# A decoder layer's last stage reordered: a new order for the last four joins, other filler counts, duplicate marks in one piece, and gates without a gather

## The chip, the cores and the metric
One core of one Trainium2 chip runs the program. The metric is its device time in microseconds, the median over executions.

## What is computed
A decoder layer on x of 2048 tokens by 256: self-attention with line coordinates, cross-attention over 1601 context rows, and a mixture of 16 experts. The change lies in the last part:

```python
x = x + _L0_xattn_ref(_layernorm(x), ctx, ctx, Wq, Wk, Wv, Wo, bo)
x = x + _L0_ffn_ref(_layernorm(x), gate_query, log_temp, w1, b1, w2, b2)
# _L0_ffn_ref
affinity = _sinkhorn(einsum('bnd,ed->ben', x, gate_query) / exp(log_temp))   # 6 rounds
gates, idx = top_k(affinity, 64)                     # 64 tokens for each of 16 experts
expert_in = take_along_axis(x[:, None], idx[..., None], axis=2)
h = gelu(einsum('becd,edf->becf', expert_in, w1) + b1)                # 256 to 1024
expert_out = einsum('becf,efd->becd', h, w2) + b2                     # 1024 to 256
out = out.at[..., idx].add(gates[..., None] * expert_out)
```

## The kernel before
**The attention part.** `build_plan` writes one list of steps, and every engine goes through that list in order and does its own share of it. A planner picks each next step from ten streams, by estimated durations and weights. The steps of normalised rows, joins and queries are one stream, `x`, whose own order `join` writes out. A join of a block of 128 tokens is: `o_turn` (TensorE turns the attention output, L1861; VectorE divides by the sums into `attn`, L1439 and L1440), `a_turn` (TensorE turns `attn`, L1865; a copy to `attn_t`, L1444), `out_proj` (TensorE, L1871; VectorE adds it to the residual rows `xb`, L1450, and takes their statistics, L1271 to L1273; GpSimd raises the variance to the power -0.5, L1022), `norm` (VectorE, L1327, then a store to DRAM), `x_turn` (TensorE, L1821; a copy to `xn_t`, L1339) and `gate` (TensorE, L1899; a copy to `logits`, L1489). TensorE's results for these go through three banks `g` in turn: a step waits until the bank of three steps before has been read. The plain copies (`a_turn`, `x_turn`, `gate`) can be VectorE's or ScalarE's, as the planner picks; ScalarE costs 50 more once the scores have begun (`act_late`), so VectorE has them. The last four blocks (12 to 15) are joined after the last attention work, when nothing else is left in the plan.

**Fillers.** `keep_busy(n)` issues n matmuls of 128x256 in f32 that nobody reads (L1787; each shows as two in the trace). They stand after each late `out_proj` (3) and ahead of TensorE's waits in the router.

**The router.** After the plan, VectorE scales the logits and makes six Sinkhorn rounds with a column sum by TensorE in each. Then 128 chunks (8 for each expert) give their 64 largest values (`best_v`, eight at a time) and their places (`find_places`, L1567); the largest of an expert's candidates give a limit, which TensorE spreads (L1947); counts per chunk (L1952, L1953) give each chunk an offset. Six steps by powers of two (L1619, L1620) shift each chunk's indices to that offset, and a matmul (L1957) sums the chunks: `idx_gather`, 64 tokens of the two experts of a pair on 128 partitions, eight pairs.

**Duplicates.** A token can be chosen by both experts of a pair, and a scatter may not add to one row twice. For each pair `mark` makes a diagonal of the indices and a row of marks (L1640, L1641), a matmul with ones adds them over the partitions (L2008, `pair_sum`), `read_sums` compares (L1648, L1650), and `place_rows` (L1656 to L1664) builds the matrix `mix` and the rows of the scatter, with an unused token for the second copy.

**The experts.** For each pair: gather 128 rows (GpSimd, L1090), turn them (L1964), hidden layer (L1977) and b1 (L1677), turn (L1990), gelu (ScalarE), output layer (L2001) and b2 (L1693), `mix` scaled by the gates (L1684) and multiplied (L2019), a copy (ScalarE, L1229), a scatter with addition to DRAM (GpSimd, L1107), each after the one before. The gates come from DRAM too: SyncE stores the affinities (L983) and GpSimd gathers 16 of them for each token (L1098), behind each gather of rows. The order at the start is written out by hand: marks 0 to 3, rows of pairs 0 and 1, hidden 0, marks 4 and 5, rows 2, marks 6 and 7, hidden 1. Weights go through eight slots; SyncE asks for experts 3 to 7 after the last stores of the joins, and for experts 8 to 15 as slots come free (w1, L793, after a pair's hidden layer has been read; w2, L798, after its output has).

## Time and profile before

| | us |
|---|---|
| median of 3 executions (1174.15 to 1175.01) | 1174.94 |
| the profiled execution's own time | 1175.17 |
| its span | 1173.4 |
| TensorE busy | 1105.5 (94%) |
| VectorE busy | 860.9 (73%) |
| ScalarE busy | 718.2 (61%) |
| GpSimd busy | 151.4 (13%) |
| mean granted TensorE clock | 0.976 |

The attention part ends at 1007.5 us of the span, so what the change touches lies in the last 166 us. Busy time of TensorE there is partly fillers. The granted clock is 1.00 at 2.4 GHz and 0.50 at 1.2 GHz.

### The profile page before, as it was taken

What the parts mean: (1) busy time and instruction counts of PE and PEld (TensorE: products, weight loads), DVE (VectorE), ACT (ScalarE), POOL (GpSimd) and SP (SyncE); (2) the same over time, 40 slices, a digit from 0 to 9 for tenths busy, and PEclk for the clock granted to TensorE, in tenths of its full rate; (3) what the DMA queues carried; (4) which work ended last, traced back from release to release, by engine and by line L of the source; (5) the groups of instructions that cost most, each with busy time, mean ns of one, the idle gap of its engine ahead of it and who ended that gap; (6) DMA issues with size and microseconds to landing.
All of it is one profiled execution on the core that took longest, in us unless ns stands there. A gap on an engine that the chain in (4) does not pass through costs nothing.

```text
span 1173.4 us, 30372 instructions
## 1 busy us (share of the span) xinstructions
PE 1105.5 (94%) x12600; PEld 525.7 (45%) x12600; DVE 860.9 (73%) x2017; ACT 718.2 (61%) x823; POOL 151.4 (13%) x260
## 2 busy tenths in 40 slices
PE   4788999999999999999999999999999999888997
PEld 2443433332432323544454456555555552467554
DVE  4888565487788878889788889788878980378631
ACT  0345567887678867677776877677785789310111
POOL 3024125112111011000001000010001000000522
PEclk9898999999999989999999999999999999998999
DMA  5113408722011000103232200111102000088696
GB/s 168 32 36 95 117 16 152 169 36 74 25 35 40 16 15 2 53 28 88 79 101 65 88 18 28 52 47 30 30 20 65 17 16 2 24 310 193 184 345 173
DMA packets 81562, 90.45 MB, mean 77 GB/s; under 512 B 18208, under 2 KB 73952, under 8 KB 81424
## 3 DMA queue, kind: packets, MB, share of 16 engines
q1 hardware_dynamic: 75264, 80.04, 23.9%
q10 hardware_dynamic: 4368, 6.29, 1.7%
q0 software_dynamic: 1792, 2.16, 1.0%
q8 instruction: 100, 1.64, 0.6%
q14 instruction: 38, 0.31, 0.1%
HBM read 73.42 MB, written 15.04 MB: 75 GB/s over the span
## 4 chain that ended last, share of the span: by engine, by line
PE 76%; DVE 11%; DMA 5%; issue 4%; ACT 2%; POOL 1%; ACTq 0%; DVEq 0%; POOLq 0%
PE po L1778 24%; PE g L1886 16%; PE scores L1754 15%; PE scores L1758 6%; PE g L1871 3%; PE g L1831 2%; ACT probs L1194 2%; DMA out<-self_region,idx_scatter 1%; DVE mx L1465 1%; PE g L1821 1%; PE g L1861 1%; DMA out<-wo_sb,idx_scatter 1%; PE scores L1787 1%; DMA out<-wxq_sb,idx_scatter 1%; PE g L1977 1%
## 5 line engine op out<-in xcount | busy, mean ns | idle before, releaser
L1194 ACT ACTIVATE probs<-scores 128x1024 f32<-128x1024 f32 (+2 forms) x736 | 677.0, 968 | 239.7 <-PE scores L1754 131.3
L1465 DVE TENSOR_REDUCE mx<-g 128x1 f32<-128x400 f32 (+1 forms) x1024 | 526.4, 567 | 86.2 <-PE g L1886 76.6
L1886 PE MATMUL g<-cross_region,even_region 96*32 96x400 bf16 (+1 forms) x4096 | 310.5, 338 | 0.4
L1754 PE MATMUL scores<-even_region,cross_region 99*32 99x512 bf16 (+1 forms) x3264 | 255.0, 379 | 2.5 <-ACT probs L1194 2.5
L1778 PE MATMUL po<-probs,cross_region 128*32 128x512 f32 (+1 forms) x1664 | 225.3, 594 | 0.8 <-ACT probs L1194 0.8
L1886 PEld LDWEIGHTS g<-cross_region,even_region 96*32 96x32 bf16 x4096 | 123.3, 95 | 182.9 <-DVE mx L1465 81.9
L1778 PE MATMUL po<-probs,self_region 128*32 128x512 f32 (+3 forms) x1280 | 152.1, 550 | 4.5 <-POOL probs L1055 3.9
L1754 PEld LDWEIGHTS scores<-even_region,cross_region 99*32 99x32 bf16 (+1 forms) x3264 | 100.9, 96 | 96.0 <-issue 42.6
L1758 PE MATMUL scores<-self_region 36*128 36x512 bf16 (+3 forms) x640 | 104.9, 360 | 7.2 <-ACT probs L1194 6.8
L1055 POOL TENSOR_SCALAR_AFFINE_SELECT probs<-probs 128x256 f32<-128x256 f32 x128 | 58.8, 468 | 276.7 <-ACT probs L1194 275.9
L1022 POOL TENSOR_TENSOR rstd<-mv,half 128x1 f32<-128x1 f32 x48 | 26.7, 556 | 518.5 <-DVE mv L1273 518.3
L1758 PEld LDWEIGHTS scores<-self_region 36*128 36x128 bf16 x640 | 26.6, 94 | 126.1 <-ACT probs L1194 76.9
L1778 PEld LDWEIGHTS po<-probs,cross_region 128*32 128x32 f32 (+1 forms) x1664 | 56.8, 110 | 24.9 <-ACT probs L1194 6.4
L1224 ACT ACTIVATE even_region<-scores 128x1024 f32<-128x1024 f32 x4 | 4.1, 1026 | 85.8 <-PE scores L1990 85.8
L1787 PE MATMUL scores<-xbo_sb,ident 128*128 128x256 f32 x190 | 51.4, 424 | 0.0
L1778 PEld LDWEIGHTS po<-probs,self_region 128*32 128x32 f32 x1280 | 30.9, 110 | 33.6 <-POOL probs L1055 13.5
L1821 PE MATMUL g<-ident,xn 128*128 128x128 f32 x96 | 21.0, 305 | 25.7 <-DVE xn L1327 25.6
L1787 PEld LDWEIGHTS scores<-xbo_sb,ident 128*128 128x128 f32 x190 | 39.5, 214 | 6.3 <-issue 0.2
L1439 DVE RECIPROCAL rsum<-g 128x16 f32<-128x16 f32 x32 | 8.2, 255 | 45.7 <-PE g L1861 45.5
L1831 PE MATMUL g<-wself_sb,xn_t 128*128 128x512 f32 x64 | 34.3, 662 | 0.1
L1450 DVE TENSOR_TENSOR xb<-g,xb 128x256 f32<-128x256 f32 x32 | 13.6, 424 | 28.1 <-PE g L1871 27.3
L1821 PEld LDWEIGHTS g<-ident,xn 128*128 128x128 f32 x96 | 10.4, 146 | 42.9 <-issue 31.0
(287 smaller groups left out, 881.3 us busy)
## 6 DMA issues: line engine op xcount, KB each, us to landing
cross_region<-in_w SPq DMA_DIRECT2D x16, 1024.0 KB, 12.8
even_region<-xq_d SPq DMA_DIRECT2D x192, 64.0 KB, 2.3
self_region<-in_w ACTq DMA_DIRECT2D x6, 1024.0 KB, 6.6
self_region<-in_w SPq DMA_DIRECT2D x6, 1024.0 KB, 13.8
cross_region<-xk_d SPq DMA_DIRECT2D x24, 200.1 KB, 8.0
xb<-in_x SPq DMA_DIRECT2D x32, 128.0 KB, 2.8
xb<-x_d SPq DMA_DIRECT2D x32, 128.0 KB, 2.4
probs<-in_w SPq DMA_DIRECT2D x4, 1024.0 KB, 13.2
```

The lines of the kernel that those rows point to most:

```text
L1022: pool.tensor_tensor(rstd[:, u % 4:u % 4 + 1], mv[:, u % 4, 1:2], half[:, 0:1], ALU.pow).then_inc(rstd_ready, 1)
L1055: pool.affine_select(out=d, in_=d, compare_op=ALU.is_ge, fill=0.0, base=0, pattern=[[0, 2], [1, P]], channel_multiplier=-1).then_inc(mask_ ...
L1194: act.activation(probs[0:rows, s % 4, :, off:], ps[s % 2][0:rows, :, off:], ACT.Exp, scale=LSCALE if QUADS[n][0] == "self" else 1.0).then_ ...
L1465: dve.reduce_max(mx[:, k % 2, b, h, c:c + 1], g[:, 0:n_keys], AX_X).then_inc(g_free, 1)
L1754: mm = pe.matmul(ps[s % 2][c:c + n_keys, a, :], k_cross[0:NS * DH + 3, h, i * P + c:i * P + c + n_keys], rhs, start=True, stop=True)
L1758: mm = pe.matmul(ps[s % 2][0:rows, a, off:], lhs, rhs, start=True, stop=True)
L1778: mm = pe.matmul(po[32 * a:32 * a + 32, off:], v[0:rows, i, h * VW:h * VW + 32], probs[0:rows, s % 4, a % 2, off:], start=(i == 0), stop=e ...
L1787: pe.matmul(ps[0][:, 0, 0:D], ident[:, :], xbo_sb[:, :], start=True, stop=True)
L1821: mm = pe.transpose(g[:, k * P:(k + 1) * P], xn[:, norm_no[u] % 2, k * P:(k + 1) * P], ident[:, :])
L1831: pe.matmul(g[:, :], xn_t[:, k, c + 1:c + 1 + P], wself_sb[:, k, 0:512], start=(k == 0), stop=False)
L1871: mm = pe.matmul(g[:, 0:D], attn_t[:, k, :], (wo_sb if step[1] == "self" else wxo_sb)[:, k, :], start=(k == 0), stop=(k == DK - 1))
L1886: mm = pe.matmul(g[q:q + 32, 0:n_keys], q_max[k % 2][0:NS * DH, h, b * P + q:b * P + q + 32], k_cross[0:NS * DH, 4 * (k % 4) + h, start:st ...
```

## The change
1. `join` has an order of its own for the last four blocks: three blocks are under way at a time, each a step behind the next, and `x_turn` of a block comes ahead of the next block's `out_proj`. The plan up to the last `pv` is the same.
2. Once the last `pv` is in the plan, the plain copies are ScalarE's, at no extra cost.
3. `keep_busy` after a late `out_proj` issues 1 for 3; ahead of the turned values it issues 18 for 15, and ahead of the chosen indices 17 for 12.
4. The marks of all eight pairs are made by one VectorE instruction in bf16 and counted by two matmuls; which indices are equal comes from eight matmuls of a broadcast column with the shifted indices, right behind the index matmul. One `read_sums` replaces two.
5. The gates are shifted and summed as the indices are (`shifted_v`, six steps by `move` and one matmul), while VectorE waits in the hidden layers. The store of the affinities and GpSimd's eight gathers of them go. One multiplication scales `mix`, for two.

```diff
@@ -111,6 +111,16 @@
     def join(kind, j):
         use = load_x(kind, j)
         s = [("x_load", kind, b, u) for b, u in use] + [("bias", kind, b, u) for b, u in use]
+        if (kind, j) == ("cross", NT - 1):
+            for n in range(len(use) + 2):
+                one, two, three = (use[n - d] if 0 <= n - d < len(use) else None for d in range(3))
+                s += [("a_turn", kind, *two)] if two else []
+                s += [("o_turn", kind, *one)] if one else []
+                s += [("norm", kind, *three), ("x_turn", kind, *three)] if three else []
+                s += [("out_proj", kind, *two)] if two else []
+                s += [("gate", three[0])] if three else []
+            return s
...
@@ -430,11 +440,13 @@
             got = place(step, free)
             if got is not None:
                 ready[name] = (step, got, weight(name, step), "DVE")
-                choices.append((name, step, got, "DVE", 0.0))
+                last = done["pv"] == n_quads and step[0] in EITHER
+                if not last:
+                    choices.append((name, step, got, "DVE", 0.0))
                 if step[0] in EITHER:
                     got = place(step, free, "ACT")
-                    choices.append((name, step, got, "ACT", W["act_late"] if ("scores", 0) in at else W["act_early"]))
-                    if got[1][-1][1] < ready[name][1][1][-1][1]:
+                    choices.append((name, step, got, "ACT", 0.0 if last else W["act_late"] if ("scores", 0) in at else W["act_early"]))
+                    if last or got[1][-1][1] < ready[name][1][1][-1][1]:
                         ready[name] = (step, got, ready[name][2], "ACT")
         assert ready, (len(plan), {n: streams[n][d] for n, d in done.items() if d < len(streams[n])})
         best = None
...
         limit = o_region[:, 1408:1416]
         counts = o_region[:, 1416:1418]
...
-        picked_affin = late_region[:, 256:256 + E // 2 * E].rearrange("p (i e) -> p i e", e=E)
+        gates = late_region[:, 256:256 + E // 2]
+        shifted_v = [even_region[:, 1024 + 2 * CAP * r:1024 + 2 * CAP * (r + 1)] for r in range(2)]
...
         idx_f, again, keep, spare = (bv_sb[:, P + 8 * r:P + 8 * (r + 1)] for r in range(1, 5))
-        marks = [attn[:, :], attn_t[:, :, :].rearrange("p k n -> p (k n)")]
+        marks = o_region[:, 1536:2048].bitcast(BF16).rearrange("p (i n) -> p i n", i=E // 2)
...
@@ -979,8 +991,6 @@
                     sp.dma_start(place[rows, :].rearrange("p (i n) -> p i n", n=D),
                                  by_parity[e][first:last, :].partition_broadcast(CAP)).then_inc(b2_loaded, 16)
-            sp.wait_ge(router_pe, 3 + SINK_ITERS)
-            sp.dma_start(affin_d.rearrange("(b p) e -> p b e", p=P), affin[:, :, :]).then_inc(affin_stored, 16)
 
             def next_w1(i):
...
+            pool.wait_ge(g_full, NG)
+            pool.memset(attn[:, 0:P // 2], BF16_ONES).then_inc(const_ready, 1)
             pool.wait_ge(picked, 2)
-            pool.wait_ge(affin_stored, 16)
             for r in range(2):
                 pool.wait_ge(xn_stored[r], 16 * TB // 2)
             for r in range(4):
@@ -1095,9 +1106,6 @@
             for i in range(E // 2):
                 if i + 2 < E // 2:
                     gather_x(i + 2)
-                pool.indirect_dma_start(
-                    picked_affin[:, i, :], None, affin_d, bass.IndirectOffsetOnAxis(idx_gather[:, i:i + 1], 0)
-                ).then_inc(gates_gathered[i], 16)
             pool.wait_ge(placed, 1)
             for i in range(E // 2):
                 pool.wait_ge(y_ready, i + 1)
...
@@ -1633,26 +1646,22 @@
             dve.wait_ge(const_ready, 15)
 
-            def mark(i):
-                if i >= 2:
-                    dve.wait_ge(pair_sums, i - 1)
-                link(dve.tensor_scalar(marks[i % 2][:, 0:P], ident[:, :], idx_f[:, i:i + 1], None, ALU.mult))
-                dve.tensor_scalar(marks[i % 2][:, P:2 * P], row_no, idx_f[:, i:i + 1], None,
-                                  ALU.is_equal).then_inc(marked, 1)
-            def read_sums(q):
-                four = slice(4 * q, 4 * q + 4)
-                dve.wait_ge(pair_sums, 4 * q + 4)
-                sums = ps[q][:, :, :].rearrange("p a b -> p (a b)").rearrange("p (i n) -> p i n", i=4)
-                link(dve.tensor_tensor(mix[:, four, 0:CAP], sums[:, :, 0:CAP],
-                                       idx_f[:, four].unsqueeze(2).broadcast_to((P, 4, CAP)), ALU.is_equal))
-                dve.scalar_tensor_tensor(out=unused[:, four, :], in0=sums[:, :, P:2 * P], scalar=0.0,
-                                         in1=row_no.unsqueeze(1).broadcast_to((P, 4, P)), op0=ALU.is_equal,
+            def mark_tokens():
+                dve.tensor_tensor(marks, row_no.unsqueeze(1).broadcast_to((P, E // 2, P)),
+                                  idx_f.unsqueeze(2).broadcast_to((P, E // 2, P)), ALU.is_equal).then_inc(marked, 1)
+            def read_sums():
+                dve.wait_ge(pair_sums, 2)
+                link(dve.tensor_tensor(mix[:, :, 0:CAP], ps[0][:, 0, :].rearrange("p (i n) -> p i n", n=CAP),
+                                       idx_f.unsqueeze(2).broadcast_to((P, E // 2, CAP)), ALU.is_equal))
+                counts_of = ps[1][:, :, :].rearrange("p a b -> p (a b)").rearrange("p (i n) -> p i n", n=P)
+                dve.scalar_tensor_tensor(out=unused, in0=counts_of, scalar=0.0,
+                                         in1=row_no.unsqueeze(1).broadcast_to((P, E // 2, P)), op0=ALU.is_equal,
                                          op1=ALU.mult).then_inc(sums_read, 1)
             def place_rows():
-                dve.wait_ge(sums_read, 2)
+                dve.wait_ge(sums_read, 1)
                 link(dve.reduce_sum(again, mix[:, :, 0:CAP], AX_X))
                 link(dve.reduce_max(spare, unused, AX_X))
                 link(dve.tensor_scalar(again, again, first_half, None, ALU.subtract))
...
@@ -1678,12 +1687,7 @@
                                       b1_sb[i % NB1][:, f * TILE:(f + 1) * TILE], ALU.add).then_inc(g_free, 1)
             def expert_out(i):
-                dve.wait_ge(gates_gathered[i], 16)
-                for e in range(2):
-                    rows = slice(CAP * e, CAP * (e + 1))
-                    last = dve.tensor_scalar(mix[rows, i, :], mix[rows, i, :],
-                                             picked_affin[rows, i, 2 * i + e:2 * i + e + 1], None, ALU.mult)
-                last.then_inc(mixed, 1)
+                dve.tensor_scalar(mix[:, i, :], mix[:, i, :], gates[:, i:i + 1], None, ALU.mult).then_inc(mixed, 1)
                 g = tail_full(dve, ("y", i))
                 if i == 0:
...
@@ -1692,19 +1696,32 @@
                     dve.wait_ge(merged, i - 1)
                 dve.tensor_tensor(y_sum[i % 2], g[:, 0:D], b2_sb[i], ALU.add).then_inc(g_free, 1)
-            for i in range(4):
-                mark(i)
+            mark_tokens()
+            for r in range(2):
+                link(dve.memset(shifted_v[r][:, 0:CAP], 0.0))
+            link(dve.scalar_tensor_tensor(out=shifted_v[0][:, CAP:2 * CAP], in0=row_no[:, 0:CAP], scalar=n_here,
+                                          in1=best_v, op0=ALU.is_lt, op1=ALU.mult))
+            link(move(shifted_v, 0))
+            link(move(shifted_v, 1))
             expert_in(0)
             expert_in(1)
-            mark(4)
-            mark(5)
-            read_sums(0)
+            link(move(shifted_v, 2))
+            read_sums()
             hidden(0)
-            mark(6)
-            mark(7)
             expert_in(2)
-            read_sums(1)
+            for k in range(3, 5):
+                link(move(shifted_v, k))
+            move(shifted_v, 5).then_inc(values_ready, 1)
             hidden(1)
+            g = tail_full(dve, "gates")
+            for e in range(2):
+                last = dve.tensor_copy(gates[CAP * e:CAP * (e + 1), :],
+                                       g[0:CAP, 0:E].rearrange("p (i e) -> p e i", e=2)[:, e, :])
+                if e == 0:
+                    link(last)
+            last.then_inc(g_free, 1)
+            dve.wait_ge(g_free, TF["gates"])
             place_rows()
             for i in range(E // 2):
                 if i + 3 < E // 2:
...
@@ -1900,7 +1917,7 @@
                                        start=(k == 0), stop=(k == DK - 1))
                 mm.then_inc(g_full, 1)
                 if kind == "out_proj" and where[step] > where["pv", len(QUADS) - 1]:
-                    keep_busy(3)
+                    keep_busy(1)
             keep_busy(6)
             g = tail_bank(pe, "col_turn")
@@ -1924,7 +1941,7 @@
             pe.transpose(g[:, 0:P], affin_r[:, 0:P], ident[:, :])
             pe.transpose(g[:, P:2 * P], affin_r[:, P:2 * P], ident[:, :]).then_inc(g_full, 1)
-            keep_busy(15)
+            keep_busy(18)
             g = tail_bank(pe, "best_t")
             pe.wait_ge(router_pe, 5 + SINK_ITERS)
             pe.transpose(g[0:CAP, 0:P], best_v, ident[:, :]).then_inc(g_full, 1)
@@ -1951,10 +1968,16 @@
             pe.wait_ge(router_pe, 7 + SINK_ITERS)
             pe.matmul(g[:, 0:2], same_expert, counts, start=True, stop=True)
             pe.matmul(g[:, 2:4], chunks_before, counts, start=True, stop=True).then_inc(g_full, 1)
-            keep_busy(12)
+            keep_busy(17)
             g = tail_bank(pe, "tops")
             pe.wait_ge(router_pe, 8 + SINK_ITERS)
             pe.matmul(g[0:CAP, 0:E], shifted[0][:, CAP:2 * CAP], same_expert[:, 0:E], start=True, stop=True).then_inc(g_full, 1)
+            pe.wait_ge(exp_done, 2 * len(QUADS))
+            for i in range(E // 2):
+                mm = pe.matmul(ps[0][:, 0, CAP * i:CAP * (i + 1)], same_expert[:, 2 * i:2 * i + 1].broadcast_to((P, P)),
+                               shifted[0][:, CAP:2 * CAP], start=True, stop=True)
+            mm.then_inc(pair_sums, 1)
 
             def expert_in(i):
...
@@ -1984,7 +2007,7 @@
                     pe.wait_ge(gelu_done, i - 1)
                 else:
-                    pe.wait_ge(sums_read, i + 1)
+                    pe.wait_ge(sums_read, 1)
                 pt = ps[i % 2][:, :, :].rearrange("p a b -> p (a b)")
                 for f in range(8):
                     mm = pe.transpose(pt[:, f * P:(f + 1) * P], h_sb[i % 2][:, f * P:(f + 1) * P], ident[:, :])
...
-            def pair_sum(i):
-                pe.wait_ge(marked, i + 1)
-                pe.matmul(ps[i // 4][:, i % 4 // 2, i % 2 * 2 * P:(i % 2 + 1) * 2 * P], ones[:, :], marks[i % 2],
-                          start=True, stop=True).then_inc(pair_sums, 1)
+            def count_marks():
+                pe.wait_ge(const_ready, 17)
+                pe.wait_ge(marked, 1)
+                for half_of in range(2):
+                    mm = pe.matmul(ps[1][:, half_of, :], ones_b, marks[:, 4 * half_of:4 * half_of + 4, :],
+                                   start=True, stop=True)
+                mm.then_inc(pair_sums, 1)
             def merge(i):
                 pe.wait_ge(mixed, i + 1)
@@ -2018,19 +2044,18 @@
                     pe.wait_ge(y_ready, i)
                 pe.matmul(po[:, 0:D], mix[:, i, :], y_sum[i % 2], start=True, stop=True).then_inc(merged, 1)
-            keep_busy(2)
-            pe.wait_ge(exp_done, 2 * len(QUADS))
-            for i in range(4):
-                pair_sum(i)
+            pe.wait_ge(o_free, len(evacs))
+            keep_busy(1, po[:, 0:D])
+            count_marks()
+            keep_busy(2, po[:, 0:D])
             expert_in(0)
             expert_in(1)
             hidden(0)
-            pair_sum(4)
-            pair_sum(5)
             expert_in(2)
-            pair_sum(6)
-            pair_sum(7)
             hidden(1)
+            g = tail_bank(pe, "gates")
+            pe.wait_ge(values_ready, 1)
+            pe.matmul(g[0:CAP, 0:E], shifted_v[0][:, CAP:2 * CAP], same_expert[:, 0:E], start=True, stop=True).then_inc(g_full, 1)
             turn_hidden(0)
             for i in range(E // 2):
                 if i + 1 < E // 2:
```

TensorE, blocks 13 to 15 of the last joins, before (L1865 turns `attn`, L1861 the attention output, L1821 the normalised rows; L1871 is `out_proj`, L1787 fillers, L1899 the gate):
```order
L1865 MATMUL g<-ident,attn 128x128 x2
L1861 MATMUL g<-ident,o_region 128x128 x4
L1871 MATMUL g<-wxo_sb,attn_t 128x256 x2
L1787 MATMUL scores<-xbo_sb,ident 128x256 x3
L1821 MATMUL g<-ident,xn 128x128 x2
L1865 MATMUL g<-ident,attn 128x128 x2
L1861 MATMUL g<-ident,o_region 128x128 x4
L1871 MATMUL g<-wxo_sb,attn_t 128x256 x2
```
TensorE at the same place, now (the same steps are L1882, L1878, L1838, L1888, L1804, L1916):
```order
L1882 MATMUL g<-ident,attn 128x128 x2
L1878 MATMUL g<-ident,o_region 128x128 x4
L1838 MATMUL g<-ident,xn 128x128 x2
L1888 MATMUL g<-wxo_sb,attn_t 128x256 x2
L1804 MATMUL scores<-xbo_sb,ident 128x256
L1916 MATMUL g<-gate_sb,xn_t 128x16 x2
L1882 MATMUL g<-ident,attn 128x128 x2
L1878 MATMUL g<-ident,o_region 128x128 x4
```
The turn of a block's normalised rows has moved from behind the next block's `out_proj` to ahead of it, and one filler stands where three stood.

TensorE between the index matmul and the second hidden layer, before (L2008 sums marks, L1964 turns gathered rows, L1977 is the hidden layer):
```order
L1957 MATMUL g<-bo_sb,o_region 64x16
L1787 MATMUL scores<-xbo_sb,ident 128x256 x2
L2008 MATMUL scores<-attn,late_region 128x256
L2008 MATMUL scores<-attn_t,late_region 128x256
L2008 MATMUL scores<-attn,late_region 128x256
L2008 MATMUL scores<-attn_t,late_region 128x256
L1964 MATMUL g<-ident,self_region 128x128 x4
L1977 MATMUL g<-self_region 64x512 x8
L2008 MATMUL scores<-attn,late_region 128x256
L2008 MATMUL scores<-attn_t,late_region 128x256
L1964 MATMUL g<-ident,wo_sb 128x128 x2
L2008 MATMUL scores<-attn,late_region 128x256
```
and now (L1978 the equal indices, L2033 the counts of marks):
```order
L1974 MATMUL g<-bo_sb,o_region 64x16
L1978 MATMUL scores<-o_region,bo_sb 128x64 x8
L1804 MATMUL po<-xbo_sb,ident 128x256
L2033 MATMUL scores<-o_region,attn 128x512 x2
L1804 MATMUL po<-xbo_sb,ident 128x256 x2
L1987 MATMUL g<-ident,self_region 128x128 x4
L2000 MATMUL g<-self_region 64x512 x8
L1987 MATMUL g<-ident,wo_sb 128x128 x2
```
All work on marks now stands ahead of the gathered rows; between the two hidden layers only the turn of pair 2 is left.

## Rows read from the trace of the kernel before
**Rows 1.** Stretches: busy time of PE, PEld, DVE, ACT, POOL, then PEclk, DMA share, GB/s
```profile
1007.50:1011.00 3.50, 1.64 (x11) 1.25 (x12) 1.37 (x5) 0.59 (x1) 0.00 (x0) 1.00 0.00 0
1011.00:1014.40 3.40, 3.40 (x9) 2.66 (x9) 1.61 (x5) 0.00 (x0) 0.30 (x1) 0.51 0.10 33
1014.40:1028.20 13.80, 10.51 (x56) 8.05 (x55) 8.20 (x25) 0.00 (x0) 1.91 (x5) 1.00 0.15 51
...
1065.60:1072.50 6.90, 6.53 (x21) 5.29 (x22) 6.08 (x21) 0.00 (x0) 0.00 (x0) 0.51 1.03 230
```
**Rows 2.** The chain of waits, last joins and two column sums (start, us, what)
```profile
1007.57 0.59 ACT o_region L1206
...
1012.69 2.23 PE scores L1787 x6
...
1018.20 0.42 DVE xn L1327
...
1020.11 1.12 PE g L1871 x4
...
1022.93 0.43 DVE xn L1327
...
1031.62 0.36 DVE wself_sb L1506
...
1042.24 0.38 PE g L1919 x2
...
1045.32 0.38 PE g L1919 x2
```
**Rows 3.** ScalarE's groups: its plain copy out of PSUM
```profile
L1125 ACT COPY xn_t<-g 128x256 f32<-128x256 f32 x6 | 2.2, 380 | 29.4 <-PE g L1821 29.3
```
**Rows 4.** Timeline around the limit: fillers (L1787), find-index (L1567), limit matmul (L1947)
```profile
1056.40 6.64 PE L1787 MATMUL scores<-xbo_sb,ident 128*128 128x256 f32 x30
...
1064.59 0.27 PE L1930 MATMUL g<-ident,o_region 128*64 128x128 f32 x1 [1.55 <-DVE o_region L1562]
...
1066.91 9.48 PE L1787 MATMUL scores<-xbo_sb,ident 128*128 128x256 f32 x30
...
1075.16 0.42 DVE L1567 FIND_INDEX8 o_region<-o_region,even_region 128x8 uint32<-128x256 f32 x1
1076.31 0.38 PE L1947 MATMUL g<-o_region,bo_sb 16*128 16x8 f32 x2
```
**Rows 5.** Timeline around the chosen indices: fillers, index matmul (L1957), second gather
```profile
1078.45 5.43 PE L1787 MATMUL scores<-xbo_sb,ident 128*128 128x256 f32 x24
...
1086.42 0.37 PE L1957 MATMUL g<-bo_sb,o_region 128*64 128x16 f32 x2 [2.54 <-DVE o_region L1620]
...
1089.00 0.96 POOL L1090 DMA_INDIRECT self_region<-xn_d,idx_gather  x1 [0.31 <-issue]
```
**Rows 6.** The chain of waits, hidden layers of the first two pairs
```profile
1092.54 3.67 PE g L1977 x16
...
1096.23 0.69 DVE even_region L1677
...
1098.78 3.58 PE g L1977 x16
```
**Rows 7.** The chain of waits, two of the eight scatters
```profile
1150.06 7.34 DMA out<-wxq_sb,idx_scatter
...
1158.15 3.79 DMA out<-wxq_sb,idx_scatter
```
**Rows 8.** DMA issues of 1148 to 1156 us (KB each, us to landing): last w2
```profile
probs<-in_w SPq DMA_DIRECT2D x1, 1024.0 KB, 12.6
```
**Rows 9.** Timeline: that load's issue, and the last pair's first output matmul
```profile
1147.27 3.40 SPq L798 DMA_DIRECT2D probs<-in_w  x1
...
1161.10 0.43 PE L2001 MATMUL g<-cross_region,self_region 128*64 128x256 f32 x1
```
**Rows 10.** Timeline of TensorE, 58 to 62 us: transposes alone
```profile
59.10 3.11 PE L1843 MATMUL g<-identb,probs 128*100 128x128 bf16 x45 [1.14 <-DVE cross_region L1432]
```

28 lines of the change are left out of this document (15 added, 13 removed).

## The prediction
> **What bounds the kernel now.** I read the granted clock by stretch, the chain of waits from the end of attention, the timeline at each place that the change touches, and the DMA issues. The plan up to the last attention step is the same, so all is decided after 1007.5 us. Four stretches follow.
>
> The last joins run from 1007.57 to 1031.62, where the router's first operation starts: 24.1 us [rows 2]. They are a chain through TensorE and VectorE, block by block: from one normalised block to the next took 4.73 us (1018.20 to 1022.93). Six filler passes stand on it for 2.23 us, because TensorE was at its low level from 1011.0 to 1014.4, after it had been half idle and done turns alone [rows 1, 2].
>
> The router follows, a VectorE chain. At one place TensorE holds it: fifteen fillers (30 passes) took 9.48 us, where another fifteen took 6.64, since the first 6.9 us of them fell into a stretch at 0.51 of the clock [rows 1, 4]. The limit matmul behind them started at 1076.31, though VectorE was through with its part and, by 1075.58, with the searches it does meanwhile.
>
> Then the indices (1086.42), the gathers and the first hidden layers, where TensorE is the bound. Between the end of the first hidden layer (1092.54 + 3.67 = 1096.21) and the start of the second (1098.78) lie 2.57 us in which it turns pair 2 and sums marks, and waits for VectorE to make them [rows 5, 6].
>
> Last, seven more pairs. Three things run level there: TensorE, the chain of scatters (7.34 us each while weights are loaded, 3.79 after), and the weights, the last of which lands at 1147.27 + 12.6 = 1159.9, when 1161.10 is the first use [rows 7 to 9].
>
> **The joins.** Two of three fillers go, four times; twelve copies go from VectorE (about 0.42 us) to ScalarE (0.38, [rows 3]), which has nothing else to do; `x_turn` goes ahead of the next `out_proj`, and `norm` ahead of its addition. `norm` then waits at the head of VectorE's queue for GpSimd's power, and the next `out_proj` for that turn, so blocks no longer overlap there: the loop is norm, turn, `out_proj`, addition, statistics, norm. From an `out_proj`'s start to its block's norm took 1022.93 - 1020.11 = 2.82; norm to `out_proj` is 0.43 + 0.13 hand-over + 0.25 for the turn. That is 3.63 a block, and 4.2 where VectorE has to divide another block first (about 0.56 of it falls into the wait).
>
> The first addition still comes at about 1012.7, since the `out_proj` before it is in the low stretch whatever is done. Its statistics give the first norm at 1012.7 + 1.7 = 1014.4, and behind a divide 1014.9, where it was 1018.20: the gain is here, from two fillers fewer at 0.43 us a pass and from the order. From there 4.2 + 3.6 + 3.6, and 2.3 for the last turn, copy, gate and copy: 1028.6. The same sums applied to the old order come out 0.4 short of 1031.5, so I take 1028.9: **-2.7 us**. Bounds: -1.2 (a loop of 4.2 in all blocks) and -3.3.
>
> All that waits for the joins comes as much earlier, the stores and so the weights of experts 3 to 7 too. ScalarE's copies stand behind nothing; its next own work is the first exponential of the router, after them all. GpSimd's new memset waits for the last gate, behind its constants, far ahead of the gathers. The six fillers behind the gates are 12 passes: 2.7 us at full speed and 5.2 at the low level. Twelve VectorE and ScalarE operations of the router come before TensorE is wanted (an estimated 4.5 us, by 0.4 each), so they cost at most a few tenths.
>
> **The fillers of the router.** Eighteen ahead of the turned values are 36 passes of 0.221 (6.64 / 30), 7.97 us, in a gap of 1064.59 - 1056.40 = 8.19: nothing. They end close to TensorE's next work, where it used to idle for 1.55 us and the clock fell a microsecond later [rows 1, 4]. If it doesn't fall, or falls for less, the next fifteen take 6.64 to about 8.3, from 1066.91: they end ahead of, or within 0.5 of, VectorE's last maximum, at about 1074.6 (two searches of 0.5 ahead of 1075.58). Then VectorE bounds the limit: searches until 1075.16 + 0.42 = 1075.58, where the limit's copy came 0.5 behind the matmul, at 1076.8 [rows 4]. **-1.1 us**; bounds 0 and -1.2. Seventeen ahead of the indices are 34 x 0.221 = 7.5, from 1078.45 to 1086.0, with 1086.42 the old start [rows 5]: nothing at full speed, with 0.4 to spare.
>
> **Marks and gates.** Ahead of the first gathered rows TensorE now does eight small matmuls (each priced by L1957, 0.3 to 0.37: 2.4 to 3.0), a filler 0.44, two bf16 matmuls of 512 (estimate 0.5, as sixteen passes of 512 took 3.67) and two fillers 0.9: from 1086.8 to 1091.0 to 1091.6. The second gather, issued at 1089.00, decides instead: the first hidden layer stands behind the turns of both pairs and started 3.5 us behind that issue, with the marks' work done by then. So it starts at 1092.3 to 1092.9, against 1092.54: nothing. Between first and second hidden layer stays the turn of pair 2 (0.3), if the bank is free: VectorE has to have done one comparison of 512 (0.7), one of 1024 (estimate twice 0.69) and one addition (0.69) after about 1093.3, so until 1096.1: just covered; without that cover up to 0.5. The gates' matmul adds 0.3 behind the second hidden layer, its six moves and `place_rows` lie beside matmuls. In sum -2.57 + 0.3 + 0.3: **-2.0 us** at the first output layer.
>
> Not all of it reaches the end. The weights have no slack but 1.2 us, and their queue starts with the first hidden layer, whose time stays; it saves the eight gathers of gates (1024 small packets) and gets its second request earlier, by estimate 1 us in sum. The scatters stay loaded: the sixth was issued when the load had just ended and took 3.79; 2 us earlier some of it is in the load and takes up to 7.34. With 3.8 for it, the end moves by 2.0, with 5 by 1.0: I take **-1.5**, bounds 0 and -2.2. Dropping the store of affinities and halving the scalings of `mix` is hidden: both lie beside matmuls.
>
> **Sum.** -2.7 - 1.1 - 1.5 = -5.3, against the profiled 1175.17: 1169.9. The median of the runs lies 0.2 lower: **1169.6 us**.
>
> **A rule on turns.** Fewer fillers leave more of the joins to transposes, and the low stretch has to end at 1014.4 for my sum. In that stretch TensorE would have `out_proj`, one filler, and six turns, where it had six filler passes. In the trace, a stretch of 45 transposes and nothing else ran and ended at full clock [rows 10]; so I hold them for work that keeps it. The Trainium skill ("TensorE: Matmul & The Clock Gate", Part 4) says that transpose mode does not count as busy in the same way, and that full speed doesn't set in for it. By that rule the joins would stay at the low level; this case's row speaks against it for bf16 transposes at full speed, and no row shows f32 turns at the low level alone.
>
> **Rivals.**
> 1. *The end is held by scatters and weights*: the 2.0 us of the first hidden layers are waited out in the seven pairs. For: the 1.2 us above, and each scatter follows the last by 0.7. Against: fewer small packets. Time 1171.1.
> 2. *The longer filler runs overrun*: the clock falls just ahead of, or in, the seventeen. A low stretch of 3.4 us lets 8 passes through for 15, 1.7 us; less 0.4 spare, +1.3, and the limit's gain may go the same way. Against: they leave less idle time before. Time 1169.6 + 1.3 + 1.1 = 1172.0.
> 3. *The joins at the low level* [rows 1], from 1011 to their end. A pass of 256 columns then takes 0.43 for 0.22, so the four of an `out_proj` add 0.8, and turns on the loop double: about 1.2 us a block, 4.8. Time 1174.4: no change.
> 4. *Slower*: the same low level outlasts the joins and gets into the Sinkhorn rounds. A round takes 1045.32 - 1042.24 = 3.08 [rows 2], its five fillers 2.2, but 4.3 at 0.43 a pass; with the column sum's 0.38 TensorE then needs 4.7, 1.6 more than a round has. It decides if the level is low when the first round begins and for more than one round: with two, 1174.4 + 3.2 = 1177.6. For: fewer fillers feed it. Against: six fillers in a row stand between joins and router, and at 1014.4, and after 1072.5, a run of fillers was followed by the full level.
>
> That the change does not do what it says I put at nothing: the new orders show it.
>
> **Numbers.** The forecast 0.55, rival 1 0.18, rival 2 0.10, rival 3 0.11, rival 4 0.06. 0.2% is 2.35 us, about what a measurement can tell from no change. Under 1172.6 lie the forecast, rival 1 and most of rival 2: faster 0.8. Rival 3 and the rest of 2 are within 0.2%: 0.14. Slower: 0.06. The range takes in the bounds of the terms, from -2.7, -1.2, -2.2 and the joins' further 0.6 down to 1168.2, and up over rivals 1 and 2 with a weak join: 1173.4.
>
> **What would show it.** In the new profile: the router's first operation at 1028 to 1030; clock 0.5 from 1011.0 to 1014.4 only, then 1.00 to 1028; the limit matmul within 0.5 us of VectorE's last maximum; the index matmul about 3.8 us earlier than 1086.42 with fillers ending ahead of it; the first hidden layer 6.1 us behind the index matmul as before, the first output layer 2 us nearer to it than before; scatters back to back. I am wrong if the clock is 0.5 through the joins, if fillers stand in the chain of waits ahead of the indices, or if the output matmuls wait for w2.

## The result, and the profile after

On the chip of the first measurement the changed kernel took 1164.99 us (median of 5 runs, 1163.39 to 1169.05), the kernel before 1174.39 (5 runs, 1172.11 to 1175.01): ratio 0.9927, 95% interval 0.9906 to 0.9949. The forecast was 1169.6, in a range of 1168.2 to 1173.4. The direction was right, the size too small, and the result lies under the range. The profiled execution of the changed kernel took 1163.39 with a span of 1161.4; the one before, 1175.17 with 1173.4.

Twelve microseconds between two spans are more than the stages I had costed could give. So the first thing to read is where they arise. This table sets single records of the two profiles against each other (start of the record, in us; "step" is what the stretch since the row above gained or lost).

| record | before | after | step |
|---|---|---|---|
| ScalarE's first exponential of attention | 68.01 | 67.46 | -0.55 |
| its last one (what lies between the two is called attention below) | 1005.37 | 999.96 | -4.86 |
| router's first turn | 1036.08 | 1028.03 | -2.64 |
| index matmul | 1086.42 | 1078.05 | -0.32 |
| first hidden layer | 1092.54 | 1083.76 | -0.41 |
| second hidden layer | 1098.71 | 1087.71 | -2.22 |
| third hidden layer | 1104.41 | 1093.48 | +0.07 |
| last pair's output layer | 1161.10 | 1150.17 | 0.00 |
| end of the last record | 1173.38 | 1161.37 | -1.08 |

Behind the last exponential, where the change is, the gain is 168.01 - 161.41 = 6.60 us. The other 5.4 lie ahead of it, in code that the change leaves alone.

**Attention.** The two kernels do the same work there in the same order, and the changed one is 0.73 us ahead as the stretches begin. Around 424 us of the kernel before (busy time of PE, PEld, DVE, ACT, POOL, then PEclk, DMA share, GB/s):

```profile
410.30:420.50 10.20, 10.20 (x136) 3.37 (x128) 8.88 (x19) 7.22 (x12) 3.26 (x8) 1.00 0.01 2
420.50:423.90 3.40, 1.91 (x18) 0.70 (x20) 1.98 (x8) 3.26 (x4) 0.00 (x0) 1.00 0.00 0
423.90:434.20 10.30, 10.30 (x78) 2.50 (x72) 5.48 (x11) 4.35 (x5) 0.00 (x0) 0.50 0.15 41
```

The changed kernel at the same work, 0.73 us earlier:

```profile
409.57:419.77 10.20, 10.20 (x136) 3.37 (x128) 8.88 (x19) 7.22 (x12) 3.25 (x8) 1.00 0.01 2
419.77:423.17 3.40, 1.91 (x18) 0.70 (x20) 1.97 (x8) 3.27 (x4) 0.00 (x0) 1.00 0.00 0
423.17:433.47 10.30, 10.30 (x130) 3.16 (x124) 9.04 (x18) 8.11 (x9) 0.00 (x0) 1.00 0.14 41
```

In both, TensorE was busy for 1.91 of 3.4 us while VectorE finished a set of maxima. Behind that its clock was at the low level (0.50, 1.2 GHz) for 10.3 us in the kernel before, and 78 matmuls went through where the changed kernel, at 1.00, had 130. So the idle time alone does not decide it: the same idle time was followed by the low level in one execution and not in the other. ScalarE's exponentials show what this costs. Before:

```profile
423.24 1.02 ACT L1194 ACTIVATE probs<-scores 128x1024 f32<-128x1024 f32 x1
425.89 1.94 ACT L1194 ACTIVATE probs<-scores 128x1024 f32<-128x1024 f32 x2 [1.63 <-PE scores L1758]
429.69 1.02 ACT L1194 ACTIVATE probs<-scores 128x1024 f32<-128x1024 f32 x1 [1.86 <-PE scores L1758]
```

After:

```profile
424.34 3.96 ACT L1202 ACTIVATE probs<-scores 128x1024 f32<-128x1024 f32 x4 [0.81 <-PE scores L1775]
429.21 1.02 ACT L1202 ACTIVATE probs<-scores 128x1024 f32<-128x1024 f32 x1 [0.91 <-PE scores L1775]
```

ScalarE waits for scores in both, but longer in the kernel before. One by one, the exponentials of the changed kernel are 0.7 us ahead until 424 us and 5.3 ahead from 435 on. Nothing of this comes back later.

**The joins.** The chain of waits after:

```profile
1009.48 0.42 DVE xn L1335
...
1013.47 0.41 DVE xn L1335
...
1014.42 0.88 PE g L1888 x4
...
1017.28 0.42 DVE xn L1335
...
1021.11 0.42 DVE xn L1335
...
1023.57 0.36 DVE wself_sb L1514
```

From one norm to the next 3.99, 3.81 and 3.83 us, against 4.73 before [rows 2]. Where a filler is still in the chain it takes 0.43 us (at 1011.31), for 2.23 before. The clock by stretch:

```profile
1003.75:1007.17 3.42, 2.76 (x10) 2.45 (x11) 1.16 (x4) 0.37 (x1) 0.00 (x0) 0.50 0.00 0
1007.17:1024.20 17.03, 10.52 (x65) 8.92 (x64) 8.25 (x27) 3.31 (x11) 3.57 (x14) 1.00 0.19 63
1024.23:1027.65 3.42, 3.19 (x8) 2.01 (x6) 2.43 (x8) 2.73 (x4) 0.39 (x2) 0.50 0.91 293
```

The low stretch [rows 1] now comes ahead of the first norm; from there the joins ran at 1.00. Turns are part of what TensorE had at 1.00, beside `out_proj`, gates and one filler a block, so these rows show that such a mixture keeps the full level, and say nothing of turns alone. As far as they go they speak, as rows 10 did, against the rule of the Trainium skill ("TensorE: Matmul & The Clock Gate", Part 4) that I had weighed.

**The router.** Its timeline around the limit:

```profile
1058.46 6.74 PE L1804 MATMUL scores<-xbo_sb,ident 128*128 128x256 f32 x30
...
1069.09 9.03 PE L1804 MATMUL scores<-xbo_sb,ident 128*128 128x256 f32 x34
...
1078.05 0.29 PE L1974 MATMUL g<-bo_sb,o_region 128*64 128x16 f32 x2
```

The limit's fillers now run at the full level (30 passes in 6.74 for 9.48, [rows 4]), and the sums behind it come 1.5 us nearer. But then the clock fell (0.50 from 1068.61 to 1072.02), the seventeen took 9.03 us instead of 7.5 and held up the index matmul, which gave 1.2 of it back: my second rival, in this execution.

**First pairs and end.** The chain of waits:

```profile
1080.54 2.75 DMA self_region<-xn_d,idx_gather
...
1083.83 3.58 PE g L2000 x16
...
1087.78 3.58 PE g L2000 x16
...
1093.55 3.58 PE g L2000 x16
1097.13 3.45 PE g L2024 x32
...
1150.24 3.60 PE g L2024 x32
1153.85 0.57 issue
1154.42 0.68 PE po L2045 x2
...
1155.78 1.55 POOL out L1115
```

Between first and second hidden layer 0.37 us are left of 2.57 [rows 6]. At the end the chain is TensorE's to its last merge, with no scatter in it, where before it ran through the scatters [rows 7]. GpSimd's timeline says the same of four in a row (in brackets its idle time, and what ended it):

```profile
1129.69 1.55 POOL L1115 DMA_INDIRECT out<-wo_sb,idx_scatter  x1 [6.05 <-ACT wo_sb L1237]
1138.06 1.55 POOL L1115 DMA_INDIRECT out<-wxq_sb,idx_scatter  x1 [6.82 <-ACT wxq_sb L1237]
1146.56 1.55 POOL L1115 DMA_INDIRECT out<-wxq_sb,idx_scatter  x1 [6.94 <-ACT wxq_sb L1237]
1151.09 1.55 POOL L1115 DMA_INDIRECT out<-wxo_sb,idx_scatter  x1 [2.98 <-ACT wxo_sb L1237]
```

Each of these waits for its own rows from ScalarE, where before each waited for the scatter ahead of it. The first scatter came as far ahead of the last output layer as before (46.4 us in both profiles).

### The profile page after: what moved, and what is told of

Its sections match the earlier page's. It is cut to its first block, busy times and chain, and to the rows that moved or that the text cites. A ratio compares the mean times of both kernels' runs of the same rounds, so it can differ in the third digit from the quotient of the medians.

```text
span 1161.4 us, 30371 instructions
## 1 busy us (share of the span) xinstructions
PE 1093.6 (94%) x12606; PEld 518.9 (45%) x12606; DVE 855.7 (74%) x1997; ACT 721.7 (62%) x835; POOL 145.7 (13%) x253
## 4 chain that ended last, share of the span: by engine, by line
PE 83%; DVE 9%; issue 3%; ACT 3%; POOL 1%; DMA 1%; ACTq 0%; DVEq 0%
PE po L1795 25%; PE g L1903 16%; PE scores L1771 15%; PE scores L1775 6%; PE g L1888 3%; PE g L1848 2%; PE g L2000 2%; PE g L2024 2%; ACT probs L1202 2%; PE g L1878 1%; PE g L1838 1%; DVE mx L1473 1%; PE g L1894 1%; PE g L1882 1%; PE scores L1804 1%
## 5 line engine op out<-in xcount | busy, mean ns | idle before, releaser
L1903 PE MATMUL g<-cross_region,even_region 96*32 96x400 bf16 (+1 forms) x4096 | 307.3, 336 | 0.4
L1838 PE MATMUL g<-ident,xn 128*128 128x128 f32 x96 | 21.0, 305 | 28.0 <-DVE xn L1335 27.9
L1804 PE MATMUL scores<-xbo_sb,ident 128*128 128x256 f32 x186 | 46.8, 403 | 0.0
L1795 PEld LDWEIGHTS po<-probs,self_region 128*32 128x32 f32 x1280 | 30.7, 109 | 34.3 <-POOL probs L1065 14.3
L1804 PEld LDWEIGHTS scores<-xbo_sb,ident 128*128 128x128 f32 x186 | 36.4, 201 | 5.1
L1838 PEld LDWEIGHTS g<-ident,xn 128*128 128x128 f32 x96 | 10.4, 146 | 44.7 <-issue 31.9
```

Source lines behind the costliest of these rows:

```text
L1795: mm = pe.matmul(po[32 * a:32 * a + 32, off:], v[0:rows, i, h * VW:h * VW + 32], probs[0:rows, s % 4, a % 2, off:], start=(i == 0), stop=e ...
L1804: pe.matmul(bank, ident[:, :], xbo_sb[:, :], start=True, stop=True)
L1838: mm = pe.transpose(g[:, k * P:(k + 1) * P], xn[:, norm_no[u] % 2, k * P:(k + 1) * P], ident[:, :])
L1903: mm = pe.matmul(g[q:q + 32, 0:n_keys], q_max[k % 2][0:NS * DH, h, b * P + q:b * P + q + 32], k_cross[0:NS * DH, 4 * (k % 4) + h, start:st ...
```

## The experiments

Runs of one group share a chip and the runs of the kernel before. The kernel before was not the same on all of them, which became the main finding, so its median stands with each group.

### First group: the stretch at 421 us, and each half of the change alone (before: 1182.28, 19 runs)

The edit at 421 us, in all four:

```
                 elif kind == "shift_turn":
+                    if step[1] == 3:
+                        for _ in range(2):
+                            pe.matmul(g[:, 0:D], ident[:, :], xbo_sb[:, :], start=True, stop=True)
                     pe.wait_ge(shift_split, step[1] + 1)
```

**Before with these fillers.** 

> The kernel before, with two filler matmuls put ahead of the fourth turn of the shifts, where TensorE stood idle twice for 0.7 us at 421 us; nothing else is changed. Theory A (a low stretch apart from the change): in the profile of before TensorE's clock is at its low level from 423.94 to 434.18 us and the exponentials behind it come 4.6 us later against the changed kernel; the fillers keep the clock up, so the time falls by 4.6 from 1174.4 to about 1169.8 and no low stretch stands between 117 and 1000 us. Theory B (the whole gain belongs to the change, the stretch is an accident of the one profiled run): the median stays at 1174.4.

Measured 1182.71 (12 runs, 1178.70 to 1184.04): no difference to before. Neither theory as written: the stretch is absent from the profile (nothing low between 116 and 1003 us), and yet the median does not fall. The profiled execution is the fastest of the twelve (1178.70, the next 1181.29), so what the others had is not on record.

**The changed kernel with them.** 

> The changed kernel with the same two fillers. Theory A: its five runs spread from 1163.4 to 1169.1 because one of them had the low stretch at 424 us; with the fillers all lie at 1163 to 1166, median 1164. The change alone is then the difference to the kernel before with the same fillers, 1169.8 - 1164 = 5.8. Theory B: the spread stays, median 1165, a run near 1169 among five, and the difference to the kernel before with the fillers is 9.4.

Measured 1165.28 (5 runs, 1164.42 to 1167.86), ratio to before 0.986 (0.9841 to 0.9879). The changed kernel is where it was; it is the kernel before that takes 8 us more here. Theory A's "all at 1163 to 1166" failed: two of the five are above 1166 with the fillers in.

**Only the joins.** 

> The kernel before with the two fillers at 421 us, and of the change only the last tile's joins: the new order, the copies by ScalarE, one filler for three. Theory A (the joins give what the sum of the prediction said, 2.7): 1169.8 - 2.7 = 1167.1, router's first operation 24.1 - 2.7 = 21.4 us behind the last copy of the attention output. Theory B (the joins give the 8 us by which the router starts earlier in the two profiles): 1161.8.

Measured 1178.57 (8 runs), 4.1 under the kernel before with the fillers: nearer to theory A's 2.7 than to 8.

**Only marks and gates.** The changed kernel with joins, copies and filler counts undone. 

> The kernel before with the two fillers at 421 us, and of the change only marks and gates, with joins, copies and the filler counts of joins and router as before. Theory A (from the index matmul on, the two profiles differ by 3.7 us, and that is this part's own): 1169.8 - 3.7 = 1166.1. Theory B (the prediction's term, part of the gain waited out at the end): 1169.8 - 1.5 = 1168.3. Theory C (the end gains only because joins come earlier too): between 1168.3 and 1169.8.

Measured 1170.42 (6 runs), 12.3 under the kernel before with the fillers. No theory had a gap of that size. The profiles tell where: from the second to the third hidden layer 13.13 us went by in the kernel before with fillers and 14.43 with the joins alone, against 5.77 with marks and gates changed and 5.70 in the first profile of before. ScalarE's timeline of the kernel before with fillers:

```profile
1104.31 1.02 ACT L1224 ACTIVATE even_region<-scores 128x1024 f32<-128x1024 f32 x1 [68.95 <-remote]
```

TensorE's:

```profile
1098.32 1.09 PE L1993 MATMUL scores<-ident,even_region 128*128 128x128 f32 x8
1105.54 1.75 PE L1993 MATMUL scores<-ident,self_region 128*128 128x128 f32 x7 [6.13 <-DVE self_region L1677]
```

And VectorE's:

```profile
1099.20 0.42 DVE L1648 TENSOR_TENSOR o_region<-scores,bv_sb 128x256 f32<-128x256 f32 x1 [3.79 <-remote]
1099.65 0.69 DVE L1650 SCALAR_TENSOR_TENSOR o_region<-scores,bv_sb 128x512 f32<-128x512 f32 x1
1104.19 1.29 DVE L1677 TENSOR_TENSOR self_region<-g,even_region 128x512 f32<-128x512 f32 x2 [3.85 <-remote]
```

ScalarE waits for eight turns whose records end at 1099.4, and starts at 1104.31, 4.9 us later (in the changed kernel 0.04: 1091.37 + 1.09 to 1092.50). VectorE stands still twice, for sums and a hidden layer that TensorE's records show done.
### Second group: what in the old stage it is (before: 1180.67, 13 runs)

**Before without the gathers of the affinities.** 

> The kernel before without the store of the affinities and the eight gathers of them; mix is multiplied by 0.5 in place of the gates, so the gates are left out of the output. In the kernel before with fillers at 421 us, 13.1 us lay between the starts of the second and the third hidden layer, where the first profile of before had 5.7, and VectorE stood still twice for 3.8 us though TensorE's records show its work done. Theory A (the small gathers among the others delay what TensorE, VectorE and ScalarE tell each other): the distance is 5.7, and the time 7 to 8 under before where before is at 1182, at most 1 under where it is at 1174. Theory B (the marks' matmuls of this place do it): the distance stays at 13, and the time within 1 of before.

Measured 1172.32 (4 runs), 8.4 under before; 5.70 us from the second to the third hidden layer. Theory A. (The store of the affinities is gone too, so this run alone does not part it from the gathers.)

**The changed kernel with those gathers put back.**

```
                     gather_x(i + 2)
+                pool.indirect_dma_start(
+                    picked_affin[:, i, :], None, affin_d, bass.IndirectOffsetOnAxis(idx_gather[:, i:i + 1], 0)
+                ).then_inc(gates_gathered[i], 16)
```

> The changed kernel with the store of the affinities and the eight gathers put back, into memory that nothing reads; each output layer's scaling waits for its gather as before. Theory A: with them 3 to 8 us come back between the first and the third hidden layer, 1165 + 3 to 8. Theory B (the marks made ahead are what saves it): 1165 to 1166, the hidden layers 3.95 and 5.8 apart as in the changed kernel.

Measured 1177.67 (10 runs). Against its relative with the old order of joins on the same chip (1165.74, below) 12 us come back, more than theory A's upper end. GpSimd's last gather in this kernel:

```profile
1098.43 0.94 POOL L1118 DMA_INDIRECT picked_affin<-affin_d,idx_gather  x1 [0.30 <-issue]
```

VectorE, adding the second hidden layer, whose matmuls end at 1091.8:

```profile
1095.27 0.69 DVE L1698 TENSOR_TENSOR self_region<-g,even_region 128x512 f32<-128x512 f32 x1 [3.68 <-remote]
1102.22 0.69 DVE L1698 TENSOR_TENSOR self_region<-g,even_region 128x512 f32<-128x512 f32 x1 [6.26 <-remote]
```

**The router's filler counts undone.** 15 and 12 for 18 and 17. 

> The changed kernel with 15 and 12 fillers ahead of the turned values and of the indices in place of 18 and 17. Theory A (as the profiles of the first runs show: 48.8 us from the first turn of the router to the index matmul in three kernels with either number, 50.0 to 50.3 where a low stretch falls into the limit's fillers): the counts themselves give nothing, within 0.5 of the changed kernel's 1165. Theory B (the prediction's term): 1.1 us more.

Measured 1168.69 (4 runs), 3.4 over the 1165.3 of the first group (another chip), more than either theory. Its profile has 4.6 us and more of this in attention (the stretch at 424 us, 422.87 to 433.11); from the router's first turn to the index matmul it has 48.91 us, and 6.66 instead of 5.7 from there to the first hidden layer. So the counts give nothing ahead of the indices, and about 1 behind them.

**The joins in the old order.** 

> The changed kernel with the last tile's joins in the order before (the copies by ScalarE and the one filler stay). Theory A (the prediction's account, in which the order and two fillers fewer give 2.7 together, and the order makes the loop 3.6 to 4.2 for 4.73 a block): 1.5 to 2.5 us more than the changed kernel. Theory B (the copies and fillers give it, the order moves only when each wait falls): within 0.5.

Measured 1165.74 (4 runs, 1164.46 to 1166.70); last exponential to router 28.94 us, inside the 28.07 to 29.80 of the new order. Theory B: the order gives nothing that can be seen. Six profiles of the new order have a low stretch like this one's (6.8 us, beginning 3.3 to 3.8 us behind the last exponential) and with it 29.2 to 29.8 us, so the old order is, if anything, 0.3 faster.

### Third group: how the delay depends on the gathers (before: 1183.03, 19 runs)

**All eight behind the gathers of rows.** 

> The changed kernel with the eight gathers of affinities put back, but all behind the gathers of rows instead of between them. Put back between them they cost 12 us (1177.7), and from TensorE's last matmul of the second hidden layer to VectorE's addition of it 9.5 us went by. Theory A (any such gather in flight beside the weights of experts 2 and 3 delays what the engines tell each other, until the last has landed): they are issued until 1098 as before, and the time stays at 1175 to 1179. Theory B (it is the rows of later pairs that were held up between them): within 2 of the changed kernel, 1165 to 1167.

Measured 1177.61 (10 runs), as between them. Theory A. (The distance called 9.5 us above is 10.4 in the trace: 1091.77 to 1102.22.)

**Four of eight.** 

> The changed kernel with four of the eight gathers of affinities put back (for pairs 0, 2, 4 and 6), between the gathers of rows. The last gather is then issued about 5 us sooner than with eight. Theory A (the delay lasts until the last gather has landed): some 5 us less than with eight, so 1171 to 1174. Theory B (a fixed stall, once such gathers and weights meet): 1176 to 1178. Theory C (a threshold of gathers): 1165 to 1166.

Measured 1175.83 (10 runs); second to third hidden layer 11.75 us for 17.17. The median lies between theories A and B; five runs are at 1172.4 to 1174.6 and five at 1177.1 to 1178.8, by a difference for which I have no trace. The profile, of the first five, is with A: counted from the index matmul, the last gather ends 4.9 us sooner than with eight (16.01 for 20.92) and ScalarE goes on 5.4 us sooner (18.49 for 23.90).

**Three fillers again in the joins.** 

> The changed kernel with three fillers behind each out_proj of the last joins, as before, for one. Theory A (two fillers fewer are what the joins gain; the order gave 0.4): 1.7 to 2.6 more than the changed kernel. Theory B (the copies by ScalarE are): within 0.7. Theory C (the fillers kept the clock up, and their loss was paid in low stretches): faster by up to 1.

Measured 1168.88 (4 runs); its profile has the stretch at 424 us, and 30.36 us from the last exponential to the router, 0.6 to 2.3 more than with one filler. Theory A by the profile. Two profiles with one filler have their low stretch where this one has it, 5.3 to 5.7 us behind the last exponential; their last norm comes 21.51 and 21.58 us behind it and this one's 23.43, so two fillers in each of four blocks are worth 1.9 us there. The median says more, and with four runs I give the difference between them to no cause.

**Fillers ahead of the joins.** 

> The changed kernel with the two fillers at 421 us, four fillers ahead of the last step of attention's values, while ScalarE makes the last exponentials (TensorE waits 2.0 us there), and one behind it, where it waits 0.75 us. In the profiles so far a low stretch of 3.4 to 6.8 us begins at 1003.8 to 1004.6, ahead of or in the joins. Theory A (those waits of TensorE bring it on): no low stretch from 900 to 1020, the router 1 to 2 us sooner, 1163 to 1164 and no run above 1166. Theory B (the joins bring it on themselves, or the fillers hold up the values): the low stretch stays or moves, 1165 to 1167.

```
                 off, rows = quad_cols(n)
+                if n == len(QUADS) - 1:
+                    keep_busy(4, bank(last_turn)[:, 0:D])
...
                 g = bank(step)
+                if step == last_turn:
+                    keep_busy(1, g[:, 0:D])
```

Measured 1165.41 (4 runs, 1163.02 to 1167.84). The low stretch is gone (none from 118 to 1025 us), and the router starts 28.24 us behind the last exponential where other profiles of the changed kernel had up to 29.34. Theory A holds for the clock and for the router; its time does not (one of four runs above 1166), and the median does not tell it from the changed kernel. No version here is shown to beat the changed kernel.

### Fourth group: the change without the delay (before: 1171.88, 29 runs, 1168.47 to 1175.09)

This chip, like the first, shows no delay in the kernel before.

**The changed kernel again.** 

> The changed kernel as it is, beside its relatives on one chip. Theory A (its gain has two parts, 6.6 us of its own work and some 8 us of delay by the small gathers where a chip shows that delay): 1165, and 15 to 18 under the kernel before where before is at 1181 to 1183. Theory B (the gain is 9.4 everywhere): 1172.

Measured 1165.15 (6 runs, 1164.76 to 1165.56), 6.7 under before, ratio 0.9948 (0.993 to 0.9966). The stages of the first two profiles gave 6.6. Part of the 6.7 is again a matter of executions: twelve of the 29 runs of before are above 1173 with a mean clock of 0.977 to 0.980, while the six lie within 0.8 us of each other; against the other 17 (median 1171.22) the difference is 6.1. Theory A's first part holds; its 15 to 18 could not be seen here.

**Before without the gathers.** 

> The kernel before without the store and the gathers of the affinities (mix is multiplied by 0.5, the gates are left out), once more and in more rounds. Theory A (the difference between it and the changed kernel is the change without the delay, 6.6 by the stages of the two first profiles): 1165 + 6.6 = 1171.6, with single runs 4 to 5 us over the rest where the low stretch at 424 us falls in. Theory B (most of it is luck with low stretches): 1168 to 1170.

Measured 1171.37 (12 runs, 1168.49 to 1174.24). Theory A. Against before it is 0.5 (ratio 0.9996, 0.998 to 1.001): without the delay the gathers cost nothing that can be told from zero, though the interval leaves room for 2 us.

**The same with fillers at 421 us.** 

> The same without the gathers, with two fillers at 421 us. Theory A (the idle of TensorE there brings the stretch on in some runs): no run more than 3 us over the lowest, and the median 0 to 2 under that of the kernel without these fillers. Theory B (the stretch comes whatever TensorE does there): the same spread and median.

Measured 1170.44 (12 runs): eleven within 1169.27 and 1172.11, one at 1175.31, the profiled one, with a low stretch at another place (159.5 to 169.7). No stretch at 424 stands in any of the six profiles with these fillers, and in six of the fourteen others (in one of them only 3.4 us of it). That speaks for theory A and does not settle it, the more so as the same idle time in the profile of the changed kernel brought no stretch; a median 0.9 lower is within the spread.

**Wide rows.** 

> The changed kernel with four gathers put back between those of rows, as in the run with half the gathers, but of 512 bytes a row instead of 64, from a copy of the input that nothing else reads (a store of 1 MB comes with it, at 1046 us). Theory A (it is gathers in flight beside the weights, whatever their size): as with half the gathers, 1172 to 1178, and about 9 us more than 5.8 between the second and third hidden layer or between first and second. Theory B (it is the small size of the rows): 1165 to 1168.

Measured 1167.05 (10 runs, five at 1164.8 to 1165.7 and five at 1168.4 to 1170.0). Without a delay it tells nothing of the rows' size. The medians of the two groups lie 4.5 apart, as much as the stretch at 424 us costs; the mean clocks (0.984 to 0.986, and 0.978 to 0.981) go with that, but the one trace is of the fast group, so the place is inferred. (The store of 1 MB was issued at 1061.4, and not at 1046.)

### Fifth group: wide rows where the delay is there (before: 1181.65, 7 runs)

> The kernel with four gathers of 512 bytes a row again, beside its fellow with 64 bytes, on one chip. If the kernel before takes 1180 or more here (the delay is there): theory A (any gather in flight beside the weights): both 1172 to 1178; theory B (the small rows): this one 1165 to 1170 and the fellow 1172 to 1178. If the kernel before takes about 1172, neither shows anything: both 1165 to 1170.

> The fellow with four gathers of 64 bytes a row. Where the kernel before takes 1180 or more: 1172 to 1178 by either theory. Where it takes about 1172, that is, where the delay is absent: 1165 to 1170, in two groups some 4.5 apart by whether the low stretch at 424 us falls in.

Measured 1173.45 with wide rows and 1172.92 with narrow ones (4 runs each); second to third hidden layer 11.69 and 12.22 us. Theory A: rows of 64 or 512 bytes make no difference that four runs can show. ScalarE and GpSimd of the kernel with wide rows:

```profile
1099.05 0.94 POOL L1122 DMA_INDIRECT rest<-xh_d,idx_gather  x1 [0.30 <-issue]
...
1102.41 1.02 ACT L1248 ACTIVATE even_region<-scores 128x1024 f32<-128x1024 f32 x1 [64.79 <-remote]
```

With this, seven profiles have the delay. In all of them ScalarE goes on 2.4 to 3.1 us behind the end of GpSimd's last gather (here 1102.41 - 1099.99 = 2.42; in the changed kernel with eight gathers 1102.35 - 1099.37 = 2.98), whether that came at 1096.4 or at 1103.5. Counted from the index matmul the last gather ends at two places only, 16 us behind with four gathers and 21 with eight, and ScalarE goes on at 18.3 to 18.5 and at 23.8 to 24.1.

## Why the prediction was wrong in size

By its own steps:

- **"The plan up to the last attention step is the same, so all is decided after 1007.5 us."** This step failed, by 4.6 us. The plan is the same, and the time is not: a low stretch of 10.2 us was in the profiled execution of before and not in that of after. I had read the clock from the end of attention only, and so took a span with that stretch in it as the base of my sum. The fourth group shows how much that is: on that chip 29 runs of before spread over 6.6 us around 1171.9. The five of the first measurement all lie in the upper half of that spread, four of them at 1174.2 to 1175.0; whether by chance or by the chip, no run tells. With 1171.9 as base my 5.3 would have given 1166.6, where 1165.15 was measured.
- **Joins, -2.7.** Right in sum: -2.64 in the two profiles, though 0.4 of it is luck. Over all profiles 30.7 to 32.7 us from the last exponential to the router with the old joins, and 28.1 to 29.8 with the new (30.4 with three fillers). I had the low stretch stay where it was, 5.6 us behind the last exponential; over the profiles it begins 3.0 to 5.7 us behind, or is not there at all, and in the profile after it came 1.9 us sooner and cost less. Where it lies as before, the last norm comes 21.51 and 21.58 us behind the last exponential for 23.76: 2.2 us. (At the router those two profiles keep 1.5 of it, as a second low stretch fell into their last operations.) The working was partly wrong too: the order, on which I built the loop, gives nothing; the fillers are 1.9 of the 2.2, and the other 0.3 is left for the copies and the order together.
- **Limit, -1.1.** Failed: 0.3 at the indices. From the router's first turn to the index matmul fifteen of twenty profiles have 48.8 to 49.0 us, with either filler count, and the five with a low stretch in the limit's or the indices' fillers have 50.0 to 50.3. The old counts had it once in eight, the new ones four times in twelve. I took a property of one execution for one of the code.
- **Seventeen fillers ahead of the indices, nothing.** Ahead of them, right. Behind them they help: with twelve, the clock fell within 0.4 to 2.4 us of the index matmul and the new marks' first hidden layer came 8.29 and 6.66 us behind the index matmul; with seventeen it did not fall there, and the layer came 5.67 to 5.76 us behind in all twelve profiles.
- **Marks and gates, -2.0 at the first output layer.** Close: -0.41 to the first hidden layer, which I had at nothing, and -2.22 to the second. The latter is the code's, for it is 3.95 from first to second hidden layer in every profile with the new marks, and 6.1 to 7.2 without.
- **"Not all of it reaches the end", -1.5.** Failed, by 2.1. From the second hidden layer to the last output layer both profiles take 62.4 to 62.5: neither the weights nor the scatters took anything back. And the end came 1.08 nearer, since the scatters left the chain: 12.28 us behind the last output layer before, 11.1 to 11.3 in the profiles of the three runs with old marks and no gathers of gates, 11.20 after. That makes -3.6 for the -1.5. My first rival and the loaded scatter had the wrong sign. This is the term with the gathers in it, which I priced as 1024 small packets of DMA time, worth part of 1 us. That their removal is what freed the end is argued from one profile of before against four; the medians of the fourth group (0.5 us) neither show nor exclude 1 us.
- **What no step had:** the small gathers beside the weights can cost 8 us by way of the engines' waits. The profile of before does not show it, so no reading of it could have priced it. It is no part of the first measurement, where ScalarE's first gelu began at 1103.42, 0.04 us behind its turns and ahead of the last gather's end at 1107.45. But on the three others where the changed kernel or a near relative ran beside before, it makes the difference 15 to 18 us.

Summed, of 6.7 us between forecast and measured spans: the stretch at 424 us 4.6, the rest of what lies ahead of the last exponential 0.8, marks, gates and end 2.1, and the limit takes 0.8 back.

## What to carry to other kernels

Before a sum is made against a profiled execution, look at the granted clock over its whole span, and ask of each low stretch whether the code or the execution put it there; a stretch in untouched code is part of the base, not of the change. Then price a removed gather or scatter not only by its bytes and its queue, but by what runs beside it, and time on more than one chip where a few per mille matter. Fillers are worth their place where TensorE waits, and can go where a chain of short matmuls has to pass them.
